# Moving the maximum-magnitude folds of the second feed-forward stage behind the rounding of each pair, on eight cores

## The reference

```python
def act_quant(x):
    scale = 127.0 / jnp.clip(jnp.max(jnp.abs(x), axis=-1, keepdims=True), 1e-05)
    q = jnp.clip(jnp.round(x * scale), -128.0, 127.0) / scale
    return x + jax.lax.stop_gradient(q - x)
def bitlinear(x, w, b):
    xq = act_quant(rmsnorm(x))
    wq = weight_quant(w)
    return jnp.einsum('bsd,fd->bsf', xq, wq) + b
h = bitlinear(x, w1, b1)              # 1024 -> 4096
h = jax.nn.gelu(h, approximate=False)
return bitlinear(h, w2, b2)           # 4096 -> 1024
```

## Time and profile before

| | us |
|---|---|
| time, median of 2 runs | 7251.7 (7236.62 and 7266.77) |
| time of the profiled execution | 7214.28 |
| span of its slowest core (core 6) | 7212.7 |
| spans of the eight cores | 7196.1 to 7212.7 |
| busy in the span: PE, DVE, ACT | 3117.9 (43%), 3793.4 (53%), 1330.5 (18%) |

### The profile page before, as it was taken

The page is one execution under the profiler, slowest core; times in us unless marked ns, Lnnn a source line. Parts: engine busy times, 40 slices in busy tenths (PEclk is TensorE's granted clock), DMA queues, the critical chain, the costliest instruction groups (busy, mean ns, idle before and its releaser), DMA issues.

```text
span 7212.7 us, 66500 instructions; the slowest of 8 cores (7196.1 to 7212.7 us)
## 1 busy us (share of the span) xinstructions
PE 3117.9 (43%) x19024; PEld 2052.4 (28%) x19024; DVE 3793.4 (53%) x8337; ACT 1330.5 (18%) x2491; POOL 5.1 (0%) x8
## 2 busy tenths in 40 slices
PE   2655556655556621142442443354254244244333
PEld 2433334433334410021321221232132132122122
DVE  2555655555656655535545545544544554554555
ACT  1111111111111100022222222222222222222221
POOL 0000000000000000000000000000000000000000
PEclk8777667776667755555665665565566566566556
DMA  6000000000000034300000000000000000000000
GB/s 115 15 16 21 15 15 17 17 21 21 15 15 17 17 119 172 102 9 0 1 15 15 15 1 15 15 1 15 15 1 15 15 1 15 15 15 1 15 12 12
DMA packets 120952, 173.96 MB, mean 24 GB/s; under 512 B 5748, under 2 KB 105236, under 8 KB 118548
## 3 DMA queue, kind: packets, MB, share of 16 engines
q1 hardware_dynamic: 115412, 152.20, 6.5%
q0 software_dynamic: 5184, 17.50, 1.5%
HBM read 145.22 MB, written 41.96 MB: 26 GB/s over the span
## 4 chain that ended last, share of the span: by engine, by line
DVE 36%; PE 32%; ACT 12%; issue 11%; DMA 7%; DVEq 2%; ACTq 0%; SPq 0%
PE psH L732 9%; DVE DH L853 8%; PE psO L867 8%; ACT HHT L742 4%; DVE MH L849 3%; DMA WQ<-f2T 3%; DVE PR L739 2%; ACT HS L748 2%; PE psRowH L751 2%; PE psRow L261 2%; PE PaA L396 2%; PE PaB L402 2%; DMA X<-xT 2%; ACT HI L837 2%; DVEq L946 2%
## 5 line engine op out<-in xcount | busy, mean ns | idle before, releaser
L751 PE MATMUL psRowH<-HS,ONEB 128*1 128x256 bf16 x512 | 184.6, 361 | 1691.8 <-ACT HS L748 1691.8
L732 PE MATMUL psH<-XQ,f1q 128*128 128x256 bf16 x4096 | 871.3, 386 | 10.0 <-ACT IABC L156 10.0
L853 DVE SCALAR_TENSOR_TENSOR DH<-MH,DH 128x512 f16<-128x512 f16 x1024 | 708.9, 692 | 109.0 <-DVE MH L849 4.6
L739 DVE TENSOR_TENSOR PR<-psH,IABC 128x256 f32<-128x256 f32 x512 | 216.7, 423 | 1005.0 <-PE psH L732 1005.0
L867 PE MATMUL psO<-HQT,f2q 128*128 128x256 bf16 x4096 | 586.4, 314 | 104.5 <-DVE HQT L858 94.9
L751 PEld LDWEIGHTS psRowH<-HS,ONEB 128*1 128x1 bf16 x512 | 40.5, 79 | 1900.2 <-issue 1900.2
L732 PEld LDWEIGHTS psH<-XQ,f1q 128*128 128x128 bf16 x4096 | 497.6, 131 | 284.6 <-issue 117.9
L867 PEld LDWEIGHTS psO<-HQT,f2q 128*128 128x128 bf16 x4096 | 451.7, 113 | 238.3 <-issue 135.7
L742 ACT ACTIVATE HHT<-PR,B1S,THR 128x256 f16<-128x256 f32 x512 | 305.3, 596 | 1120.1 <-DVE PR L739 1119.9
L837 ACT ACTIVATE HI<-Y1H 128x512 int32<-128x512 f16 x256 | 161.1, 629 | 1721.8 <-DVE Y1H L833 1706.9
L762 DVE TENSOR_TENSOR MX<-MX,HHT 128x256 f16<-128x256 f16 x496 | 145.1, 293 | 520.9 <-ACT HHT L742 520.9
(11 more groups left out here) (160 smaller groups left out, 4520.7 us busy)
## 6 DMA issues: line engine op xcount, KB each, us to landing
WQ<-f1T SPq DMA_DIRECT2D x16, 2048.0 KB, 8.6
WQ<-f2T SPq DMA_DIRECT2D x64, 512.0 KB, 3.3
X<-xT SPq DMA_DIRECT2D x16, 1024.0 KB, 5.6
xoh<-XOUT SPq DMA_DIRECT2D x16, 1024.0 KB, 4.4
XO<-xoh SPq DMA_DIRECT2D x16, 1024.0 KB, 5.7
outT<-XO SPq DMA_DIRECT2D x16, 1024.0 KB, 4.4
xqh<-XQS SPq DMA_DIRECT2D x128, 64.0 KB, 1.6
XQ<-xqh SPq DMA_DIRECT2D x16, 512.0 KB, 6.8
```

The costliest lines, as they stand in the source:

```text
L732: mm = e.matmul(pH[:], f1q[:, c, fc * 128:(fc + 1) * 128], XQ[:, c, :], start=(c == 0), stop=(c == NCHUNK - 1))
L739: f=lambda e, pH=pH, PR=PR: e.tensor_tensor(out=PR[:], in0=pH[:], in1=IABC[:], op=ALU.mult))
L751: f=lambda e, fc=fc, hsq=hsq: e.matmul(psRowH[:, 0, :], ONEB[:], hsq[:], start=(fc == 0), stop=(fc == F2CHUNK - 1)))
L853: f=lambda e, s=s: e.scalar_tensor_tensor(out=DH[:], in0=MH[:], scalar=-s, in1=DH[:], op0=ALU.mult, op1=ALU.add))
```

## The change

The folds are taken out of `p2_m6_chunk` and become a function of their own, `p2_m6_folds`, with the same instructions. For tile 0 it is called behind each chunk as before. For every later tile the folds of chunks 2g and 2g+1 of tile `it+1` are issued behind the tail of pair g of tile `it`, for all 16 pairs. Nothing else is moved, and no instruction is added or taken away.

```diff
         ctx.op("pe", r=[khs, "onesbf"], w=["ph:row"],
                f=lambda e, fc=fc, hsq=hsq: e.matmul(psRowH[:, 0, :], ONEB[:], hsq[:],
                                                     start=(fc == 0), stop=(fc == F2CHUNK - 1)))
+
+    def p2_m6_folds(it, fc):
+        hs_ = hslot(it, fc)
+        kHc = "HHT:%d" % hs_
         if fc == 0:
             ctx.op("dve", r=[kHc], w=["MX2"],
                    f=lambda e, hs_=hs_: e.tensor_copy(out=MX2[:], in_=HHT[:, hs_, :]))
@@
     for fc in range(F2CHUNK):
         p2_m6_chunk(0, fc)
+        p2_m6_folds(0, fc)
@@
             p2_pair_tail(it, g)
+            if it + 1 < NT:
+                p2_m6_folds(it + 1, 2 * g)
+                p2_m6_folds(it + 1, 2 * g + 1)
             if g == 13:
                 p2_invh_bcast(it)
```

## The result

| | us |
|---|---|
| changed kernel, median of 11 runs | 7449.0 (7414.5 to 7554.9) |
| kernel before, median of 10 runs | 7217.3 (7212.7 to 7266.8) |
| ratio | 1.0296, 95% interval 1.0268 to 1.0324 |
| forecast | 7424, range 7340 to 7480; slower 0.79 |

The forecast holds, and its direction too. Its size, +172 us or 2.4%, was short: the ratio stands for +193 to +234 us. What follows finds the missing part in stage 2.

The account below looks back on a forecast made before the run. No engine was taken to bound everywhere: PE sets run-up and pairs 0 to 3, DVE the ends of pairs 4 to 11. Terms 82.9 + 66.6 + 25.1 - 2.5 = +172 us on median 7251.7 give 7424, range 7340 to 7480.

Parts of the forecast that it names:

- pairs 4 to 11: Middle pairs, tiles 1 to 14: second chunk's folds give back 0.74, four folds add 1.48; +0.74 us each, +82.9.
- pairs 12 to 14: Late pairs without chunks, tiles 0 to 14: nothing leaves, four folds add 1.48 us each, +66.6.
- pair 15 to the stats: Tile end, tiles 0 to 14: stats follow HQT by 2.01 us instead of 0.34; +1.67 each, +25.1.
- tile 0, pairs 0 to 11: No evacuation waits for gelu here, so the tail starts 1.69 us earlier against 1.48 added; -0.21 each, -2.5.
- run-up: Eight chunks a tile: folds lie hidden beside PE's work, its chain of 4.24 us a turn stays; 0.
- pairs 0 to 3 of tiles 1 to 14: Set by PE; the added folds fall in front of 5.09 us of DVE idle time; 0.
- group of four folds: Between HQT and the next head on DVE: 2.01 us where 0.53 stood, third fold's step taken as 0.53; +1.48.
- Rival (a): Four folds between HQT and head are cheaper, towards 1.29 us, third step 0.34; +137 us, 1.9%; chance 0.12.
- Rival (b): Middle pairs: writing PR1 doesn't hold the evacuation back, tail starts 0.95 us earlier; +66 us; chance 0.05.
- Rival (c): Run-up is paced by DVE, so folds and waits leaving it count 193 us; -21 us; chance 0.03.
- Rival (d): Folds behind the tail lose overlap with one or both neighbours, 0.19 each in 184 groups; +207 to +242; chance 0.08.
- +214: Sum in us if semaphore waits cost nothing extra: a fold group costs 1.86, middle pairs give back 0.93.

Follow-up runs that it names:

- x1: Changed kernel with the evacuation's product written to PR0 instead of PR1; 1.0111 of the kernel before.
- x5: Changed kernel with the folds of pairs 12 to 15 between head and tail instead of behind the tail; 1.0113 of the kernel before.
- x7: Changed kernel, folds moved to where DVE idles: run-up, between a pair's two scalings, last chunk's in pair 12 between head and tail; PR1 kept; 0.9827 of kernel before.
- x2: Changed kernel with the scaling's wait for PE made last instead of first; 1.0217 of the kernel before.
- x3: Changed kernel with folds of chunks 0 to 7 back in the run-up, those of 8 to 31 behind the tail of their own pair; 1.0095 of kernel before.

## Why the prediction was right, and which term was missed

The prediction's reading of the stretches held, term by term (before and the change, core 6, 14 tiles unless said):

| term | forecast | measured |
|---|---|---|
| pairs 4 to 11 (112) | +82.9 | 6.09 x 14 = +85 |
| pairs 12 to 14 (45) | +66.6 | 4.36 x 14, and 4.43 in tile 0: +65.5 |
| pair 15 to the stats (15) | +25.1 | 1.66 x 15 = +24.9 |
| tile 0, pairs 0 to 11 | -2.5 | -1.9 |
| run-up (15) | 0 | 1.05 x 14, and 0.95 in tile 0: +15.7 |
| pairs 0 to 3 of tiles 1 to 14 | 0 | 0.67 x 14 = +9.4 |
| sum | +172 | +199 |

That the forecast time of 7424 lies only 25 us from the measured 7449 is in part luck. It starts from 7251.7, the median of two runs, and ten runs gave 7217.3; from there the same sum gives 7389, 60 too low.

The steps of the group of four folds (+1.48 forecast, 9.33 - 7.87 = +1.46 measured as medians), the 0.74 given back by the second chunk, and the wait for gelu that stays through PR1 were right. By the table x1 took the wait away and found 0.91 a pair (7.31 / 8), x5 the late groups and found 1.46 (4.38 / 3), and x7 the second chunk's folds and found 0.72 (5.76 / 8).

The step that failed is the zero for the run-up and for pairs 0 to 3: "PE's chain of 4.24 stays as it is". It was argued from the work on the path, which indeed did not change. What was left out is the order of the program itself: it shows three waits at the scaling in the place of one, and the text had written down that a wait already made is not made again, without asking who makes it once the fold is gone. The size fits a count: of the eight steps from the first scaling of a run-up to the ninth, seven got two waits more behind PE's and so 0.138 us each. That makes 0.97 of the 1.05 us measured, and x2 gave back 0.95. In pairs 0 to 3 one step of 0.138 and seven of 0.069 make 0.62 of the 0.67 measured, but x2 gave back only 0.33 there, in the stretch that differs by 0.4 between cores, so how much of its 9 us is owed to the waits stays open. Over stage 2 x2 gave back 22 of the 27 us by which the forecast fell short.

Rival (a) fell on the third fold's step, 0.53. Rival (b) was made true by x1. Rival (c), that DVE paces the run-up, fell in x3. Rival (d) fell on the steps of 0.35 and 0.34 beside the group. The rule of the Trainium skill (VectorE: DVE Perf Modes, The DRAIN you can't avoid) that a semaphore between two instructions costs nothing extra doesn't hold here: in the changed kernel the same fold took 0.34 to its successor without a wait and 0.53 with one. The same section of the Trainium skill adds that a next instruction "that is not held starts earlier". The 0.34 agrees with that, and the prediction left it out when it worked out +214 by that section.

The signs foretold were there: heads 15.0 and 9.3 apart, the wait of 0.87 ahead of the evacuation, none in tile 0. Two were not: the turn of the run-up, foretold at 4.24, was 4.37, and pairs 0 to 3, foretold unchanged, were 0.67 longer.

What stays open is small: stage 2 grew by 200 us on core 6, which is 2.8% of 7217. The ratio of the runs is 2.96%, with 2.8% inside its interval. On the eight cores stage 2 grew by 198 to 220 us, most on cores 2 and 3 of the die with the lower clock. Whether the rest of the ratio is more than the spread of the slowest of eight cores was not tried.

## What to carry to other kernels

Idle time ahead of an instruction is a gain only if the engine doesn't wait for something else right behind it: of the 494 us of waiting for gelu that left the folds 97.6 came back ahead of the evacuation and waiting for PE grew by 655, while work that had been hidden was put on the path. In a program in strict order, place small work between an engine's own unavoidable waits (here the two scalings), not behind the chain that feeds the next step, and look which buffer carries the next wait. And when an instruction is moved away, list the waits that it had made for those behind it: they reappear on the path, and where several are made, the one that comes last in time should stand last in the order.

## What the runs showed of the hardware

The order of waits at one DVE instruction is worth time. With the same three waits, the scaling started 0.24 us behind the end of PE's products when PE's wait stood first, and 0.11 behind it when it stood last, as it does with a single wait. A wait that is long fulfilled still costs about 0.07 us once the late one has come (medians 0.106, 0.175 and 0.244 with none, one and two behind PE's; x2 had 0.107 throughout). Beside that, a row of four short instructions on DVE fits into another engine's 1.55 us at no cost: the tail came 1.99 behind the head instead of 1.97.
